# Routing and the first experts of a mixture done beside the last head of the attention before it

## The reference

```python
# layer 0, attention: 16 heads of 128, rotary, causal softmax
q, k, v = x @ Wq.T, x @ Wk.T, x @ Wv.T
scores = einsum("bthd,bshd->bhts", rope(q), rope(k)) * scale
y = einsum("bhts,bshd->bthd", softmax(causal(scores)), v) / 3.0 @ Wo.T
# layer 0, feed-forward: 32 experts of width 96, the best four of each token
probs = softmax(x @ router_w.T); rw, sel = top_k(probs, 4); rw = rw / rw.sum()
out = sum over e of  w_tok[e] * ((silu(x @ gate_w[e].T) * (x @ up_w[e].T)) @ down_w[e].T)
```

## Time and profile before

| | us |
|---|---|
| median of 3 runs | 1721.63 (1718.85 to 1722.12) |
| the profiled execution | 1727.47 |
| its span, first to last instruction | 1725.7 |
| PE busy | 1548.3 (90%), mean granted clock 0.968 |
| DVE, ACT, POOL busy | 1174.9, 926.7, 706.0 |
| first run's last PE instruction ends | 237.09 |
| first mixture block | 237.4 to 388 |

### The profile page before, as it was taken

One profiled execution on the slowest core, in us unless ns is written; L12 is line 12 of the kernel. 1 busy time (PEld: TensorE's weight loads), 2 busy tenths in 40 slices (PEclk: granted clock), 3 DMA queues, 4 the chain that ended last, 5 costly groups with the idle time before them and its releaser, 6 DMA issues. The chain is left out here.

```text
span 1725.7 us, 26051 instructions
## 1 busy us (share of the span) xinstructions
PE 1548.3 (90%) x8400; PEld 1218.3 (71%) x8400; DVE 1174.9 (68%) x2492; ACT 926.7 (54%) x2012; POOL 706.0 (41%) x686
## 2 busy tenths in 40 slices
PE   6999869988999898899989989879999897999898
PEld 4777658876787688745645546568887785888787
DVE  5888847775787678889979974346666444665633
ACT  5555526664665466576656542146565444565543
POOL 5999842315222233159819852112212232212222
PEclk9999979998999999999999998899999998999999
DMA  4212122102111222050023000011111212111111
GB/s 127 77 59 78 37 90 92 65 1 67 45 49 54 78 93 89 19 205 1 1 92 132 1 6 1 7 47 50 33 49 55 74 37 69 41 49 43 64 57 48
DMA packets 34333, 98.37 MB, mean 57 GB/s; under 512 B 6388, under 2 KB 11256, under 8 KB 32072
## 3 DMA queue, kind: packets, MB, share of 16 engines
q1 hardware_dynamic: 33064, 90.95, 15.8%
q0 software_dynamic: 1184, 6.37, 1.1%
HBM read 96.12 MB, written 1.18 MB: 56 GB/s over the span
## 5 line engine op out<-in xcount | busy, mean ns | idle before, releaser
L910 POOL TENSOR_TENSOR head_low<-head,head_high 128x512 fp32r<-128x512 f32 x64 | 81.8, 1278 | 460.4 <-ACT head_high L900 459.7
L1809 POOL TENSOR_TENSOR experts_low<-experts,experts_high 128x1536 fp32r<-128x1536 f32 (+1 forms) x64 | 144.6, 2263 | 285.2 <-ACT experts_high L1755 161.8
L1262 ACT ACTIVATE probs<-banks,neg_max 128x512 f32<-128x512 f32 (+3 forms) x256 | 131.4, 526 | 151.3 <-DVE neg_max L1172 151.3
L2348 POOL TENSOR_TENSOR rings<-du,bc_rows 128x512 f32<-128x512 f32 x124 | 155.3, 1271 | 20.7 <-DVE banks L2274 13.3
L2274 DVE TENSOR_TENSOR_SCAN banks<-banks,rings 128x512 f32<-128x512 f32 x128 | 156.0, 1220 | 2.6 <-ACT banks L2172 1.8
L219 PE MATMUL banks<-experts_high,xnT_high 128*128 128x384 f32 (+1 forms) x384 | 139.8, 364 | 6.1 <-POOL experts_low L1809 6.1
L1474 ACT ACTIVATE act_out<-banks 128x256 f32<-128x256 f32 (+2 forms) x112 | 47.5, 424 | 179.9 <-PE banks L219 179.6
L1506 DVE SCALAR_TENSOR_TENSOR hidden<-banks,weight,act_out 128x96 f32<-128x96 f32 (+1 forms) x192 | 62.7, 368 | 117.0 <-ACT act_out L1474 116.5
L2066 PE MATMUL banks<-rings,ident 128*128 128x512 f32 x256 | 126.5, 607 | 17.6 <-DVE rings L2297 17.2
L219 PE MATMUL banks<-experts_high,xnT_low 128*128 128x384 f32 (+1 forms) x384 | 137.8, 359 | 0.0
L219 PE MATMUL banks<-experts_low,xnT_high 128*128 128x384 f32 (+1 forms) x384 | 137.7, 359 | 0.0
(11 more groups left out here) (287 smaller groups left out, 4729.7 us busy)
## 6 DMA issues: line engine op xcount, KB each, us to landing
head<-in_heads SPq DMA_DIRECT2D x64, 384.0 KB, 3.1
experts<-in_experts SPq DMA_DIRECT2D x16, 1152.0 KB, 5.1
bc_rows<-bc_rows SPq DMA_DIRECT2D x30, 512.0 KB, 6.2
experts<-in_experts SPq DMA_DIRECT2D x16, 768.0 KB, 4.3
values<-in_values SPq DMA_DIRECT2D x32, 256.0 KB, 3.1
coef<-in_spline_coef POOLq DMA_DIRECT2D x8, 768.0 KB, 4.6
idx<-in_lut_idx SPq DMA_DIRECT2D x16, 134.0 KB, 2.1
x<-in_x SPq DMA_DIRECT2D x2, 512.0 KB, 4.4
```

Of the source, the lines that this page charges most:

```text
L1262: last = nc.scalar.activation(prob_tile(i), score_tile(i), ACT.Exp, bias=neg_max[:, i:i + 1], scale=QK_SCALE, accum_out=row_sum[:, i:i + 1])
L1809: nc.gpsimd.tensor_tensor(parts[gpar][1][:, columns], raw[gpar][:, columns], parts[gpar][0][:, columns].bitcast(FP32), ALU.subtract)\
L2348: nc.gpsimd.tensor_tensor(inflow[:, step % INFLOWS], du[:, c], B_of(n), ALU.mult)\
```

## The change

`MixtureStart` is a new class that holds the buffers of group 0, the router and its vectors, and the steps of a mixture's beginning; `mixture` makes one itself, or takes one (`start`). For the first run it is made ahead of the attention block and handed to it in an `Ahead`:

- SP: the router's load stands at the end of the block's first loads; the load of group 0 behind the load of head 15.
- PE: the router's product behind the last head's scores, in place of the missing projection.
- ACT: both high parts of group 0 (1536 and 768 columns) before the last head's exponentials; the exponentials of the logits behind its `store_y`.
- DVE: `choose` behind the last head's scaling; `weigh` (the four normalizing instructions) behind its `store_low`.
- POOL: both low parts of group 0 behind its last work for the heads, after a wait for `probs_ready` of head 15.

In the first mixture block SP then issues: table, table chunk 0, group 1, chunk 1. DVE takes the table's differences behind item 0's gate. ACT makes gate/up of every odd group one item later than before: at c = 0 of its own pair of groups, not at c = 7 of the pair before (and, for group 1, not ahead of item 0). In the other three mixtures only two issues of SP change places: both groups' loads, then chunk 0, then chunk 1.

To make room, the first run borrows buffers: its value parts lie in sequence 1's transposed parts, its `qkT` in `xn`.

```diff
+    def lend_heads(self):
+
+        high, low = self.xnT_parts_of[1]
+        qkT = self.xn[:].rearrange("p t d -> p (t d)").rearrange("p (w c) -> p w c", w=2)
+        return [[high[:, i], low[:, i]] for i in range(2)], qkT
 ...
     # attention.sync
         for h in range(HEADS - LOOP, HEADS - 2):
             reload(h, h % LOOP, h // 2)
+        if ahead and ahead.load_first:
+            ahead.load_first(sp)
 ...
     # attention.vector, at its end
         store_low(HEADS - 1)
+        if ahead and ahead.weigh:
+            ahead.weigh(dve)
 ...
     # attention.scalar, at its end
         if ahead:
             ahead.first_high(act)
         exponentials(HEADS - 1)
-        if ahead:
+        if ahead and ahead.second_high:
             ahead.second_high(act)
         store_turned(HEADS - 1)
         store_y(HEADS - 1)
+        if ahead and ahead.exponent:
+            ahead.exponent(act)
 ...
     # attention.gpsimd, at its end
         low_wo(pool, HEADS - 1, 1)
+        if ahead and ahead.low_first:
+
+            pool.wait_ge(probs_ready.sem, probs_ready.at(HEADS))
+            ahead.low_first(pool)
 ...
+class MixtureStart:
 ...
+    def load_first(self, sp):
+        sp.dma_start(self.raw[:], head_rows(self.m.dram[f"experts{self.layer}"], 0))\
+          .then_inc(self.experts_loaded[0].sem, 16)
 ...
+    def exponent(self, act):
+        act.wait_ge(self.logits_in.sem, self.logits_in.at(1))
+        self.m.nc.scalar.activation(self.expd[:], self.expd[:], ACT.Exp).then_inc(self.exp_in.sem, 1)
 ...
+    def first_high(self, act):
+        nc, GU = self.m.nc, self.GU
+        act.wait_ge(self.experts_loaded[0].sem, self.experts_loaded[0].at(16))
+        nc.scalar.activation(self.parts[0][:, 0:GU], self.raw[:, 0:GU], ACT.Copy).then_inc(self.gu_high.sem, 1)
+        nc.scalar.activation(self.parts[0][:, GU:], self.raw[:, GU:], ACT.Copy).then_inc(self.down_high.sem, 1)
+
+    def low_first(self, pool):
+        nc, GU = self.m.nc, self.GU
+        for columns, high, split in ((slice(0, GU), self.gu_high, self.gu_split),
+                                     (slice(GU, self.WIDTH), self.down_high, self.down_split)):
+            pool.wait_ge(high.sem, high.at(1))
+            nc.gpsimd.tensor_tensor(self.parts[1][:, columns], self.raw[:, columns],
+                                    self.parts[0][:, columns].bitcast(FP32), ALU.subtract).then_inc(split.sem, 1)
 ...
     # mixture.sync
+        if table and started:
+            table.start(sp)
+            table.load(sp, 0, 0)
+        for g in range(2):
+            if started and g == 0:
+
+                continue
+            load(g, g)
+        if table and not started:
+            table.load(sp, 0, 0)
         if table:
-            table.start(sp)
-        for g in range(2):
-            load(g, g)
-            if table:
-                table.load(sp, g, g)
+            table.load(sp, 1, 1)
 ...
     # mixture.vector
         gate(dve, 0, 0, 0, 0)
+        if table and started:
+            table.first(dve)
 ...
     # mixture.scalar
+            if c == 0 and started:
+                high_gu(act, 2 * pair + 1, 1, 16 * (pair + 1))
             if c == 1:
                 high_down(act, 2 * pair + 1, 1)
             if not final:
 ...
-                if c == 7:
+                if c == 7 and not started:
                     high_gu(act, 2 * pair + 3, 1, 16 * (pair + 2))
 ...
     # hybrid_stack_kernel
+                    start = MixtureStart(m, 0, m.local(rows_ctx))
 ...
-                        first, heads = attention(m, 0, layer_ctx, spline, norm_here=True)
+                        ahead = Ahead(start.load_router, start.route, start.begin_vector, start.choose,
+                                      start.first_high, None, start.load_first, start.low_first, start.exponent,
+                                      start.weigh)
+                        buffers = HeadBuffers(m, 0, layer_ctx, m.lend_heads())
+                        first, heads = attention(m, 0, layer_ctx, spline, ahead, buffers, norm_here=True)
```

More of the change, by code:

```diff
@@ L1531, in mixture @@
+def mixture(m, layer, ctx, table_at=None, buffers=None, rows=None, norm=None, start=None):
     nc = m.nc
-    E, TOP = (E0, TOP0) if layer == 0 else (E3, TOP3)
     shape = Hidden(GROUPS, F0, (P, P, P), 4, ACT.Silu) if layer == 0 else Hidden(GROUPS, F3, (P, P), 1, ACT.Gelu)
     F, R = shape.cols, len(shape.rows)
[L1535 to L1538, removed]
@@ L1539, in mixture @@
[L1539 to L1541 removed]
+    experts_dram = m.dram[f"experts{layer}"]
     ITEMS = NT * GROUPS
@@ L1545, in mixture @@
     LOOPS = (ITEMS - TAIL) // UNROLL
-    EP = E + 8 - TOP
-    merged = buffers is not None
+    merged, started = buffers is not None, start is not None
     sb = m.local(ctx)
-    GU = KD * 2 * F
-    raw = [sb(f"experts{i}", [P, GU + R * D]) for i in range(2)]
-    parts = [[sb(f"experts_{part}{i}", [P, GU + R * D], FP32R) for part in ("high", "low")] for i in range(2)]
+    if not started:
+        start = MixtureStart(m, layer, sb)
+    GU, weight = start.GU, start.weight
+    experts_loaded, gu_high, gu_split, down_high, down_split, logits_in = (
+        start.experts_loaded, start.gu_high, start.gu_split, start.down_high, start.down_split, start.logits_in)
+    raw = [start.raw, sb("experts1", [P, start.WIDTH])]
+    parts = [start.parts, [sb(f"experts_{part}1", [P, start.WIDTH], FP32R) for part in ("high", "low")]]
     gu = [[a[:, 0:GU].rearrange("p (k w f) -> p k w f", k=KD, w=2) for a in pair] for pair in parts]
     dn = [[a[:, GU:].rearrange("p (r d) -> p r d", d=D) for a in pair] for pair in parts]
[L1555 to L1562, removed]
     scale_of = lambda g, t, e: weight[:, t, bass.ds(g * shape.experts + e, 1)]
@@ L1608, in sync @@
                     table.load(sp, g + 2, gpar)
-    def route(pe):
-        if layer == 0:
-            pe.wait_ge(loaded.sem, loaded.at(16))
-        else:
-            pe.wait_ge(scaled_router.sem, scaled_router.at(1))
-        for t in range(NT):
-            for k in range(KD):
-                last = nc.tensor.matmul(m.banks[:, 3, t * E:(t + 1) * E], m.xnT[:, k, t * P:(t + 1) * P],
-                                        router[:, k], start=k == 0, stop=k == KD - 1)
-        last.then_inc(routed.sem, 1)
     def tensor(pe):
         pe.sem_inc(added.sem, 1)
-        if not merged:
-            route(pe)
+        if not merged and not started:
+            start.route(pe)
         def step(n, c, pair):
@@ L1785, in step_act @@
                     high_down(act, 2 * pair + 2, 0)
-                if c == 7:
+                if c == 7 and not started:
                     high_gu(act, 2 * pair + 3, 1, 16 * (pair + 2))
-        if not merged:
-            first_high(act)
+        if not merged and not started:
+            start.first_high(act)
             second_high(act)
-        act.wait_ge(logits_in.sem, logits_in.at(1))
-        nc.scalar.activation(expd[:], expd[:], ACT.Exp).then_inc(exp_in.sem, 1)
+        if not started:
+            start.exponent(act)
         activate(act, 0, 0)
@@ L1814, in gpsimd @@
         low_down = lambda g, gpar: low(slice(GU, GU + R * D), down_high, down_split, g, gpar)
-        low_gu(0, 0)
-        low_down(0, 0)
+        if not started:
+            start.low_first(pool)
         low_gu(1, 1)
@@ L1844, in close @@
             s.close(GROUPS)
-    ahead = Ahead(load_router, route, begin_vector, choose, first_high, second_high)
+    ahead = Ahead(start.load_router, start.route, start.begin_vector, start.choose, start.first_high, second_high)
     return Stage(close, sync, tensor, vector, scalar, gpsimd), ahead, (added, ITEMS + 1)
```

192 lines of the change are left out of this document (118 added, 74 removed).

## The result

| | before | after |
|---|---|---|
| median of 7 runs, us | 1721.63 (1718.27 to 1728.87) | 1707.5 (1700.2 to 1709.66) |
| ratio to before | 1 | 0.9905, 95% interval 0.9884 to 0.9925 |
| profiled execution, us | 1727.47 | 1707.5 |
| its span, us | 1725.7 | 1705.7 |
| first block's last matmul ends | 237.09 | 236.63 |

A turn is PE's transpose of one item's hidden tile, L1452 before and L1471 after; the 32 of the first mixture serve as its clock here. The change makes the kernel faster by 0.95% (0.75 to 1.16%). The difference of the medians is 14.1 us, that of the two profiled spans 20.0. Of the kernel before there is one profile, 5.8 us above its median, so how much its own rows vary isn't known.

What follows compares the result with a forecast made beforehand. PE was taken to wait in the hand-over hole from 237 to 249, with the mixture behind it a PE stage. 14.0 + 0 - 1.0 + 1.1 = 14.1 us off the median 1721.6 gave 1707.5, range 1702 to 1712.

Steps and rivals of the forecast that it cites:

- 1, the hole: Hand-over from attention block to first mixture: first gate/up at 237.4 instead of 249.00, shorter start; gain 14.0 us.
- 2, the last head: Work put beside the last attention head fits in idle times: cost 0; bounds, gain 3 to loss 3.5 us.
- 3, group 1: First mixture's start: group 1's load comes late, stalling PE and ACT's queue; loss 1.0 us, bounds nothing to 4.
- 4, odd groups later: First mixture: copies at c = 0 free the predicated copies but masks are held; +2.0 at group 3, -0.9 at group 5.
- rival A: Masks at c = 0 pass, both stalls go: +3.9 + 1.2 for +1.1, gain 18.1, 1703.5 us; chance 0.22.
- 5, the rest: Other mixtures' exchange of two load issues, and the borrowed buffers: no effect, 0.
- B: Slow start: group 1 lands at 247 (4.0 for 1.0) or clock stays low (2.4); 1710.3 us; chance 0.20.
- D: No change: PE waits at the mixture block's start for something unnamed, the hole stays; 1721 us; chance 0.02.
- C: Late odd groups make PE stop at each of four groups, costing 21 us; 1728 us; chance 0.03.

Runs made afterwards that it cites:

- e0_after: The kernel after once more, unchanged, for a second trace: 1709.63 us, ratio 0.9919 to the kernel before.
- e9_after_again: The kernel after once more, unchanged, for a third profile: one execution, 1709.42 us.
- e3_no_wait: The kernel after without POOL's wait for the scaled probabilities ahead of group 0's low parts: 1714.03 us, ratio 0.9944 to the kernel before.
- e5_experts_only: The kernel after with only group 0's load, high and low parts ahead, routing back in the mixture block: 1715.17 us, ratio 0.9948 to before.
- e1_odd_back: The kernel after with odd groups' gate/up copies back at c = 7, group 1's behind item 0's activation: 1717.31 us, ratio 0.9957 to before.
- e4_route_only: The kernel after with only routing ahead, group 0's load, high and low parts back in the mixture block: 1722.28 us, ratio 0.9997 to before.

## Why the prediction was right, and where its terms were not

The time was forecast at 1707.5 us and came out there, to the digit by luck: the ratio's interval alone leaves 13 to 20 us of gain for the forecast's 14.1, and steps 3 and 4 came near their sizes with parts that weren't forecast (below). For the profiled execution the same sum gave 1713.4, and that one took 1707.5. The steps:

**1, the hole (+14.0): right.** First product 0.47 us after the block's last matmul, where 0.3 was expected, at clock 1.00. Turn 0 came 14.2 us earlier than before, in e0_after 13.7 and in e9_after_again 13.0; item 2's first matmul, forecast for 241.8, started at 241.62, 242.11 and 242.77. What the step did not say is how the 14 divides: at turn 0 routing alone is worth nothing and the experts alone 8.0. The prediction's sentence that POOL released PE in the hole already held the first of these.

**2, the last head (0): right, within its bounds.** Copies, routing and two held instructions of `choose` are where they were put, and the weights were ready 0.7 us before the block's end. The transposes took 1.58 instead of 2.39, the gain at the clock that was left out (granted 0.79 in 227.70:229.30), but this too differs between executions: 1.42 in e0_after, and 2.39 at clock 0.50 in e9_after_again. The exponentials came 1.1 us later (223.47 for 222.41). They waited for the row maxima and not for the copies, which left 0.41 us of the 1.0 to spare; the head before was already late (ACT stored its y at 220.06 for 218.29), for a cause that was not followed up. The block ended 0.46 us earlier than before, in e0_after 0.03 later and in e9_after_again 0.69 later. The cover is thin: e3_no_wait moved POOL's parts forward by nothing but the missing wait and lost 4.4 us.

**3, group 1 (-1.0): right in two profiles of three, by another split.** In the first profile of after its load, issued at 237.76, let ACT start at 243.35, and turns 1 to 3 lost 0.2 us. In e0_after it was 244.85 and the loss (4.11 - 3.48) + (4.08 - 3.50) = 1.2; in e9_after_again 245.54 and 1.2. The load took 5.6 us in the first and 6.6 in the other two, where the prediction had 5.7 from the earlier trace rows; in the other kernels with the same order of loads it took 6.5 to 6.9, and 5.5 in e5_experts_only, so the longer one is the usual case.

**4, odd groups later (+1.1): the mechanism of rival A in the profile of after, the forecast's at group 3 in two others, where the size came out by luck.** By the first profile the masks passed, and turns 8 to 12 took 13.90 us for 17.88: +4.0, as rival A had it. In e0_after and e9_after_again the masks of group 3 were held, as step 4 said, but for a delay of 1.0 to 1.1 us and not 1.9. Group 5's passed each time. Taken over all turns at which a stall falls (4 to 6, 8 to 14, 16 to 20), before needs 54.4 us, the profile of after 50.3, e0_after 53.4 and e9_after_again 53.5: gains of 4.1, 1.0 and 0.9 for the forecast's 1.1. In e0_after the 1.0 isn't made as the forecast's 1.1 was (2.0 at group 3 less 0.9 at group 5). Group 3's turns 8 to 12 gained 2.7 and group 5's turns 16 to 20 0.75, 3.5 together. What brought this down to 1.0 is what the step left out: the even groups' copies go on being held, turns 4 to 6 lost 2.0 and turns 12 to 14 0.5. The stall before turn 5 is 2.7 us in all three profiles (2.2 before), and in e0_after PE's clock falls behind it. Windows of e0_after and then of after at that place, clock in the third column from the end:

```profile
257.00:261.00 4.00, 2.67 (x18) 2.35 (x16) 3.53 (x6) 0.60 (x2) 2.10 (x1) 1.00 0.01 2
261.00:264.00 3.00, 1.75 (x13) 1.78 (x14) 3.00 (x13) 0.89 (x2) 0.00 (x0) 0.90 0.04 8
264.00:268.00 4.00, 4.00 (x19) 3.96 (x19) 0.31 (x1) 2.92 (x7) 1.48 (x1) 0.65 0.13 34
```

```profile
257.00:261.00 4.00, 1.41 (x10) 1.12 (x9) 3.52 (x12) 0.49 (x1) 0.59 (x1) 1.00 0.01 2
261.00:264.00 3.00, 3.00 (x23) 3.00 (x22) 1.80 (x8) 2.40 (x5) 0.00 (x0) 1.00 0.16 46
264.00:268.00 4.00, 4.00 (x29) 3.93 (x28) 2.45 (x10) 3.72 (x9) 1.85 (x1) 1.00 0.02 4
```

The same 2.7 us of waiting before turn 5 left the clock at 1.00 in the one execution and took it to 0.65 in the other, where the matmuls of turn 5 to 6 needed 5.08 us for 3.51. In e9_after_again they needed 5.08 too. What makes the difference is open.

**5, the rest (0): not tested by itself.** No stall of the kernel after leads to it.

**The sum** of what was measured is 14.2 - 0.2 + 4.1 = 18.1 in the first profile (18.0 read at turn 31), 13.7 - 1.2 + 1.0 = 13.5 in e0_after (13.4 read) and 13.0 - 1.2 + 0.9 = 12.7 in e9_after_again (12.6 read), and the medians differ by 14.1 in both sets of runs. The forecast priced the course that two of the three profiles took at group 3; the first profile shows the other. Its 18.1 is rival A's gain in the sum but not in the terms: A had 5.1 for step 4 and -1.0 for step 3, measured were 4.1 and -0.2. The remaining 2.0 us between that profile's 18.0 and the spans' 20.0 lie behind this block and weren't followed up.

**The rivals.** A is not another kernel but another course of the same one. B's load, 4.0 us for 1.0, didn't come: group 1 was there at 244.85 in e0_after and 245.54 in e9_after_again, not at 247, and cost 1.2. Nor did its slow clock at the start, PE was at 1.00 from 237 to 257. D, the hole stays, was refuted by the first product 0.47 us behind the block's end. C was refuted: the late copies never made PE wait for a group, and e1_odd_back, with the early ones, is 7.7 us slower. The rule of the Trainium skill that the prediction weighed (SBUF — State Buffer, "Who interferes with whom": the first to issue has the shared pair for its instruction, the other fully blocks) agrees with the held scaling (6.48 us) and with POOL ahead of the masks (4.14). By itself it doesn't say who follows when DVE's next instruction and a waiting POOL one want the pair together, and just that decides between A and the forecast: here it was the fourth mask when POOL came just behind the third's start, and mostly POOL before that.

## What to carry to other kernels

Where the next step waits for two chains, move the longer one first, and count on the shorter one only together with it: here the longer alone brought 8.0 us at turn 0, the shorter alone nothing, both 13.0 to 14.2. A wait of one engine on another's signal can cost nothing and win a lot where the two share a port: POOL told to start 1.3 us later than it could (258.98, ACT's copy being done at 257.63), behind a burst of DVE, was worth, with the earlier signal of DVE that it needs, 9.6 us (1701.85 to 1692.25), against 14 for the whole hand-over. When two profiles of one program differ by microseconds, go through them turn by turn before looking for a cause in the code: here 4.6 us were a load 1.0 us longer, a clock that fell in one and not in the other, and a meeting of two engines within 0.3 us. And a total that agrees proves no term: step 4's 1.0 for 1.1 was a gain of 3.5 and a loss of 2.5 that the forecast hadn't priced.

## What the hardware showed that was not expected

- Four masks back to back kept GpSimd's subtraction out to the end of the burst each time it came 0.43 us behind the first (0.35 us of waiting), eight half masks also at 0.26 (0.6 to 0.8 us), while a predicated copy 0.06 to 0.27 us behind the low part's start took 3.75 to 3.78 us for 0.46.
- The outcome of a meeting 0.26 to 0.30 us after the burst's start differs between executions and within one (e4_route_only), and is worth 3.3 us of DVE's time each time (4.22 for 0.92) and 1.0 to 1.4 of PE's.
- The same wait of PE (2.7 us before turn 5) is followed by a granted clock of 0.65 in one execution and of 1.00 in another.
